# GNN kernel, two attention passes: a third message buffer, and a group's three messages ahead of the next scores

## The reference, cut to what matters

```python
def gat_conv(x, src, dst, W, a_src, a_dst, b):      # HEADS = 8, HEAD_DIM = 32
    h = (x @ W).reshape(N, HEADS, HEAD_DIM)
    e = (h * a_src).sum(-1)[src] + (h * a_dst).sum(-1)[dst]
    e = where(e > 0, e, 0.2 * e)
    m = segment_max(e, dst)
    ex = exp(e - m[dst])
    out = segment_sum(h[src] * ex, dst) / segment_sum(ex, dst)
    return out.reshape(N, HEADS * HEAD_DIM) + b
```

## Time and profile before

| what | value |
|---|---|
| median of 3 runs | 8510.54 us (8506.95 to 8514.32) |
| the profiled execution's own time | 8508.31 us |
| its span, first to last instruction | 8506.5 us |
| granted TensorE clock, mean | 0.829 of full speed |
| first attention pass, start of its first differences | 5810.10 us |
| second attention pass, end of its last combine | 8466.37 us |

### The profile page before, as it was taken

One profiled execution on the slowest core, in us unless ns is written; L12 is line 12 of the kernel. 1 busy time (PEld: TensorE's weight loads), 2 busy tenths in 40 slices (PEclk: granted clock), 3 DMA queues, 4 the chain that ended last, 5 costly groups with the idle time before them and its releaser, 6 DMA issues. The chain is left out here.

```text
span 8506.5 us, 114405 instructions
## 1 busy us (share of the span) xinstructions
PE 6048.5 (71%) x25008; PEld 4478.6 (53%) x25009; DVE 5060.9 (59%) x9534; ACT 2517.1 (30%) x5684; POOL 4108.7 (48%) x4374
## 2 busy tenths in 40 slices
PE   3877787846366667699999999945666664666665
PEld 1446666644244445366666666634555553555554
DVE  4249999952433332466666666655666665666666
ACT  0135555514000001233333333333333332333332
POOL 0037777710377772144444444406666652666663
PEclk9989989878687775899999999966777776777777
DMA  3258888850233331243434334314444442444443
GB/s 119 110 180 261 261 262 260 259 124 4 69 105 105 105 105 37 96 120 113 118 117 119 117 117 120 113 36 138 140 138 127 136 120 74 132 133 137 135 124 91
DMA packets 440380, 1100.31 MB, mean 129 GB/s; under 512 B 102512, under 2 KB 177365, under 8 KB 439479
## 3 DMA queue, kind: packets, MB, share of 16 engines
q0 software_dynamic: 249344, 763.23, 32.1%
q1 hardware_dynamic: 190636, 333.56, 11.8%
HBM read 1014.51 MB, written 81.94 MB: 129 GB/s over the span
## 5 line engine op out<-in xcount | busy, mean ns | idle before, releaser
L765 POOL DMA_INDIRECT st_rows<-g_table,st_stage_idx x1632 | 1561.0, 956 | 881.3 <-issue 457.0
L2475 PE MATMUL st_psM<-st_msg,st_hot 128*128 128x273 f32 x3264 | 958.0, 454 | 310.8 <-DVE st_msg L2322 234.6
L872 POOL DMA_INDIRECT st_rows<-kv_table,st_stage_idx x832 | 841.0, 1011 | 347.6 <-issue 242.5
L705 POOL DMA_INDIRECT st_rows<-p_table,st_stage_idx x816 | 855.3, 1048 | 303.0 <-issue 220.4
L2475 PEld LDWEIGHTS st_psM<-st_msg,st_hot 128*128 128x128 f32 x3264 | 711.3, 223 | 512.9 <-issue 200.1
L765 POOL DMA_INDIRECT st_rows<-h_table,st_stage_idx x816 | 776.6, 952 | 244.5 <-issue 236.3
L1601 DVE TENSOR_TENSOR st_pre<-st_psP,st_rows 128x512 f32<-128x512 f32 x816 | 523.9, 683 | 534.0 <-PE st_psP L1692 393.1
L1698 PE MATMUL st_psC<-st_w,st_rT 128*128 128x256 f32 x3264 | 814.6, 392 | 0.0
L1698 PEld LDWEIGHTS st_psC<-st_w,st_rT 128*128 128x128 f32 x3264 | 587.2, 190 | 373.7 <-ACT st_rT L1659 212.3
L1508 PE MATMUL st_psM<-st_rows,st_hot 128*128 128x256 f32 x1632 | 506.1, 479 | 381.9 <-DMA st_rows<-h_table,st_stage_idx 187.8
L1654 ACT ACTIVATE st_gate<-st_pre 128x256 f32<-128x256 f32 x816 | 340.3, 417 | 1283.9 <-DVE st_pre L1601 1283.9
(11 more groups left out here) (400 smaller groups left out, 11397.9 us busy)
## 6 DMA issues: line engine op xcount, KB each, us to landing
st_dst_row<-in_dst_row SPq DMA_DIRECT2D x310, 512.0 KB, 5.8
kv_table<-st_rows_out SPq DMA_DIRECT2D x25, 1560.0 KB, 5.6
st_ea<-in_ea SPq DMA_DIRECT2D x103, 256.0 KB, 3.8
st_rows<-g_table,st_stage_idx POOLq DMA_INDIRECT x1632
st_pens<-pen_table SPq DMA_DIRECT2D x208, 72.0 KB
st_rows<-kv_table,st_stage_idx POOLq DMA_INDIRECT x832, 5.0
st_rows<-h_table,st_stage_idx POOLq DMA_INDIRECT x816
st_rows<-p_table,st_stage_idx POOLq DMA_INDIRECT x816, 3.7
```

Of the source, the lines that this page charges most:

```text
L705: pool.indirect_dma_start(out=rows[:, u * SLOTS + j, :], out_offset=None, in_=table, in_offset=bass.IndirectOffsetOnAxis(ap=stage_idx[:, u ...
L765: pool.indirect_dma_start(out=rows[:, slot, j, :], out_offset=None, in_=table, in_offset=bass.IndirectOffsetOnAxis(ap=stage_idx[:, g, u * ...
L872: pool.indirect_dma_start(out=rows[:, slot, j, :], out_offset=None, in_=kv_table, in_offset=bass.IndirectOffsetOnAxis(ap=stage_idx[:, g, u ...
L2475: last = nc.tensor.matmul(out[:, 0:MSG_W], onehots[:, j, :], msg[:, n, j, :], start=(j == 0), stop=(j == SLOTS - 1))
```

## The change

`st_msg` gets a third buffer, one for each supertile of a group, and `st_diff` a second. On DVE, the differences of the next group come ahead of the third combine, and all three messages of the next group behind it, ahead of the next edge scores; the loop's branch stands behind the messages. On ACT, the weights of the next group stand behind the factors of the third supertile, with a wait for the one-hots ahead of them (they share a PSUM bank with the columns that `make_hot` reads), and the three pairs of message columns stand together at the head of a group. On PE, the second scatter follows the first, then come the transposes of the scores, and the extras' sums move back: that of the first supertile behind the transposes, that of the second behind `turn_back`. After each `expand` a matmul of two zero columns carries the semaphore, so that DVE needs no count of extras there. `work_of` is split in two: DVE loads the blocks of three supertiles at once at the head of a group, and the bounds of an extra's loop only where there is one.

```diff
+    def blocks_of(eng, row, count=1):
+
+        _, values = nc.values_load_multi_w_load_instructions(
+            work[0:1, ds(row, count), 2:4], engines=[eng.engine], min_val=0, max_val=NS * NB,
+            skip_runtime_bounds_check_because=BOUNDED)
+        return [(values[2 * n], values[2 * n + 1]) for n in range(count)]
...
-            msg = st.sb("msg", [P, 2, SLOTS, MSG_W])
+            msg = st.sb("msg", [P, U, SLOTS, MSG_W])
-            diff = st.sb("diff", [P, SLOTS, U, H3])
+            diff = st.sb("diff", [P, 2, SLOTS, U, H3])
+            zeros = st.sb("zeros", [P, 2], F32R)
...
-                        _, x1, _, _ = work_of(dve, U * q + U)
                         dve.wait_ge(S["expanded"], START + U * q + U)
-                        dve.wait_ge(S["x_expanded"], START + x1)
...
-                    def combine(s, n, ahead, ahead_u):
-                        x0, x1, b0, more = work_of(dve, s + 1)
+                    def combine(s, n, ahead, ahead_u, block):
+                        b0, more = block
...
-                        n = slot % 2
-                        dve.wait_ge(S["summed"], START + s - 1)
-                        v.tensor_tensor(msg[:, n, :, GAT_W:GAT_W + H3], group_view(psW)[:, :, u, :],
+                        dve.wait_ge(S["summed"], START + s - 2)
+                        v.tensor_tensor(msg[:, u, :, GAT_W:GAT_W + H3], group_view(psW)[:, :, u, :],
...
-                    def group(i, g, ahead):
+                    def differences(i, g):
                         q = 2 * i + g
+                        dve.wait_ge(S["back_ps"], START + q + 1)
+                        hold(dve, held)
+                        v.tensor_tensor(diff[:, g, :, :, :], et[:, :, :, :], group_view(psW), ALU.subtract).then_inc(S["diffed"], 1)
+
+                    def early_messages(i, g):
+                        messages(i, g, 0)
+                        messages(i, g, 1)
+                        messages(i, g, 2)
+
+                    def group(i, g, ahead, blocks):
                         s = 6 * i + U * g
                         link.turn()
-                        dve.wait_ge(S["back_ps"], START + q + 1)
-                        v.tensor_tensor(diff[:, :, :, :], et[:, :, :, :], group_view(psW), ALU.subtract).then_inc(S["diffed"], 1)
-                        messages(i, g, 0)
                         if ahead:
-                            dve.wait_ge(S["diffed"], START + q + 1)
+                            dve.wait_ge(S["diffed"], START + 2 * i + g + 1)
                             edge_scores(i + g, 1 - g)
-                        messages(i, g, 1)
-                        combine(s, g % 2, s + U, 0)
-                        messages(i, g, 2)
+                        combine(s, g % 2, s + U, 0, blocks[0])
                         if ahead:
                             segment_maxima(i + g, 1 - g)
-                        combine(s + 1, (g + 1) % 2, s + U + 1, 1)
-                        combine(s + 2, g % 2, s + U + 2, 2)
+                        combine(s + 1, (g + 1) % 2, s + U + 1, 1, blocks[1])
+                        if ahead:
+                            differences(i + g, 1 - g)
+                        combine(s + 2, g % 2, s + U + 2, 2, blocks[2])
+                        if ahead:
+                            early_messages(i + g, 1 - g)
 
                     v.memset(NODE[:, :, :], 0.0)
                     v.memset(best[:, :, :], -BIG)
+                    v.memset(zeros[:, :].bitcast(F32), 0.0).then_inc(S["zeroed"], 1)
...
+                    differences(0, 0)
+                    early_messages(0, 0)
                     with dve.Fori(0, TURNS - 1) as i:
                         for g in range(2):
-                            group(i, g, True)
...
                     def message_columns(i, g, u):
                         slot = U * g + u
                         s = 6 * i + slot
-                        act.wait_ge(S["combined"], START + s - 1)
+                        act.wait_ge(S["combined"], START + s - 2)
                         hold(act, held)
-                        nc.scalar.activation(msg[:, slot % 2, :, MSG_W - 1], first[:, ds(s * SLOTS, SLOTS)], ACT.Copy, scale=RAISE)
+                        nc.scalar.activation(msg[:, u, :, MSG_W - 1], first[:, ds(s * SLOTS, SLOTS)], ACT.Copy, scale=RAISE)
                         nc.scalar.activation(
-                            msg[:, slot % 2, :, 0:GAT_W].rearrange("p j (h c) -> p j h c", h=H3)[:, :, :, HW3 - 1],
-                            diff[:, :, u, :], ACT.Exp).then_inc(S["msg_cols"], 1)
-
-                    def group(i, g, ahead):
+                            msg[:, u, :, 0:GAT_W].rearrange("p j (h c) -> p j h c", h=H3)[:, :, :, HW3 - 1],
+                            diff[:, g, :, u, :], ACT.Exp).then_inc(S["msg_cols"], 1)
+
+                    def weights(i, g):
+                        act.wait_ge(S["diffed"], START + 2 * i + g + 1)
+                        hold(act, held)
+                        act.wait_ge(S["onehot"], START + 6 * i + U * g + U)
+                        nc.scalar.activation(group_view(psU), diff[:, g, :, :, :], ACT.Exp).then_inc(S["weights"], 1)
+
+                    def group(i, g, ahead, last=False):
                         q = 2 * i + g
                         s = 6 * i + U * g
-                        act.wait_ge(S["diffed"], START + q + 1)
-                        nc.scalar.activation(group_view(psU), diff[:, :, :, :], ACT.Exp).then_inc(S["weights"], 1)
                         message_columns(i, g, 0)
                         message_columns(i, g, 1)
+                        message_columns(i, g, 2)
                         make_factors(s)
                         if ahead:
                             make_hotrow(q + 2, 0)
-                        message_columns(i, g, 2)
                         if ahead:
                             make_hotrow(q + 2, 1)
+                        make_factors(s + 1)
+                        if ahead:
                             make_hotrow(q + 2, 2)
-                        make_factors(s + 1)
                         make_factors(s + 2)
+                        if not last:
+                            weights(i + g, 1 - g)
                         if ahead:
                             make_extra_hotrows(q + 2)
 
...
-                        bring(hotrow[:, u, :, :], block_number(b0), u == 0).then_inc(S["expanded"], 1)
+                        bring(hotrow[:, u, :, :], block_number(b0), u == 0)
                         with pe.If(more):
+                            x0, x1 = extras_of(pe, s + 1)
                             with pe.Fori(x0, x1) as x:
                                 pe.wait_ge(S["x_hotrow"], START + x + 1)
                                 bring(xhotrow, block_number(b0 + 1 + x - x0), False).then_inc(S["x_expanded"], 1)
-
-                    def sum_up(out, onehots, n):
+                        at = u * 2 * H3
+                        nc.tensor.matmul(psE[:, at:at + 2], hotrow[:, u, 0, :], zeros[:, :], start=False, stop=True,
+                                         skip_group_check=True).then_inc(S["expanded"], 1)
...
                         scatter(s, 0, g % 2)
-                        scatter_extra(s, g % 2)
+                        scatter(s + 1, 1, (g + 1) % 2)
                         if next_scores:
                             turn_scores(q + 1)
-                        scatter(s + 1, 1, (g + 1) % 2)
-                        scatter_extra(s + 1, (g + 1) % 2)
+                        scatter_extra(s, 0)
                         scatter(s + 2, 2, g % 2)
                         if next_scores:
                             turn_back(q + 1)
-                        scatter_extra(s + 2, g % 2)
+                        scatter_extra(s + 1, 1)
+                        scatter_extra(s + 2, 2)
                         if next_rows:
                             for u in range(U):
                                 expand(q + 2, u)
 
+                    pe.wait_ge(S["zeroed"], START + 1)
```

More of the change, by code:

```diff
@@ L738, in work_of, with extras_of @@
         return at_least_zero(eng, values, NS * NB)
+    def extras_of(eng, row):
+        _, values = nc.values_load_multi_w_load_instructions(
+            work[0:1, ds(row, 1), 0:2].squeeze(1), engines=[eng.engine], min_val=-1, max_val=NS * NB,
+            skip_runtime_bounds_check_because=BOUNDED)
+        return at_least_zero(eng, values, NS * NB)
+    def blocks_of(eng, row, count=1):
+        _, values = nc.values_load_multi_w_load_instructions(
+            work[0:1, ds(row, count), 2:4], engines=[eng.engine], min_val=0, max_val=NS * NB,
+            skip_runtime_bounds_check_because=BOUNDED)
+        return [(values[2 * n], values[2 * n + 1]) for n in range(count)]
     def block_number(b):
@@ L2303, in combine @@
                         with dve.If(more):
+                            x0, x1 = extras_of(dve, s + 1)
                             with dve.If(more - 1):
@@ L2387, in make_extra_hotrows @@
```

(20 more changed lines are left out.)

24 lines of the change are left out of this document (13 added, 11 removed).

## The result

The changed kernel takes 8309.51 us (median of 4 runs, 8301.32 to 8314.22) against 8508.75 (8499.17 to 8514.32): a ratio of 0.9766, 95% interval 0.9749 to 0.9783. The forecast was 8312.

A forecast was written before the change was run, and what follows sets the result against it. A chain between engines, not any engine's load, was taken as the bound. Group heads and bodies summed to 1078.9 us per 32 groups, 84 and 112 us less; 8508.3 − 196 = 8312, own range 8270 to 8350, stated range 8235 to 8420.

The forecast's parts named there:

- The sum: Both passes: 32 groups take 1078.9 us each, 84 and 112 us less, together 196, giving 8312.
- head and body: Parts of a group's period: previous third combine to first combine (forecast 11.9 to 18.7 us), then to third combine (13.3 to 20.0).
- The stalls: Loop branches of DVE and ACT: stalls taken as gone or covered; a 3.3 us stall costs at most 3.3.
- rival B: Loop branches: ACT's and DVE's second stalls stay, costing 65 us in the first pass, 15 in the second; 8390, chance 0.17.
- a rule whose block size was wrong: Loop branches: targets outside two blocks of 256 instructions must be fetched; ACT's loops and DVE's second would fit, ending stalls.
- The messages: Group's head: three messages hide behind PE's 6.43 us first scatter; two extra ahead of edge scores cost 4.84 us.
- C: Gathered rows come late: DVE waits 4 us in half of the 68 groups, +136 us, about 8448; chance 0.07.
- E: PE's clock: the second scatter stays slow, 6.43 us not 3.86; at 3.9 us a group, 8575; chance 0.05.
- F: PE idles less, so the first scatter takes 3.86 us, 2.6 less; half the gain taken, 8246; chance 0.10.
- D: Extras' sums come later, 69 us in 14 first-supertile groups; the head's gain is given back, about 8500; chance 0.05.
- c + 20.0: Body of a group with a first-supertile extra: third combine's end of the span, 20.0 us after first combine c.

The follow-up runs named there:

- after_fit34: The changed kernel with 34 idle increments ahead of ACT's loop in the second pass; 8305.56 us, ratio 0.9761 to the kernel before.
- after_pe_order: after_fit34 with PE's old order of sums, extras and transposes; 8201.84 us, ratio 0.9641 to the kernel before.

## Why the prediction was right

**The sum.** The forecast was 1078.9 us for 32 groups in either pass; 1076.83 and 1086.92 were measured. Walking one group through four engines with durations of the earlier trace rows gave the periods to 0.1 us (no extra), 0.9 (first supertile), 0.8 (second) and 0.2 (third), with the errors of head and body mostly of opposite sign. That the sum is off by only 2.1 us in the first pass is luck in part: the seven groups of the first kind were forecast 6.0 us too long together, the eight of the second 6.7 too short.

**The stalls** (rival B). ACT's went from the first pass and DVE's second one from the second, as the sum took them. In the second pass a new one of ACT came, 39.5 us of "issue" that the forecast had excluded, by a rule whose block size was wrong. It cost some 7 us (1086.92 with it, 1080.09 without it in after_fit34), with 3 us of difference between the same runs in the first pass, where neither has it. Three heads of groups with an extra of the second supertile took 17.4 to 17.6 us with the stall and 15.4 without.

**The messages** are hidden behind the first scatter's 6.43 us as said: where nothing is ahead the head is 12.4 us and DVE waits 1.3 of them (forecast: PE at 11.9, DVE at 11.75). With an extra ahead it mostly waits 3.4 to 4.6 us, where up to 6.4 was forecast.

**C** (late rows): 12.0 us in 2 places; the slack was there. **E and F** (PE's rate): pairs take 6.43 + 3.86 as before, the clock is 0.76; neither shows.

**D was half right, and the sum hid it.** The mechanism named there is real: an extra's sum that comes 4.9 us later in the 14 groups with one of the first supertile. It was priced at 69 us, which makes 8381 and not the "about 8500" of that rival; after_pe_order measured 60 in these groups, and 44 more in the groups without such an extra, whose scans wait for the transposes behind the second scatter, which no rival priced. The forecast's c + 20.0 held the cost, but against the kernel before, whose body was 19.0 on the mean, it looked like 1 us. With the rest of the change in place and PE's old order it is 15.2.

Part by part the 199 us are: -78 for stalls of the kernel before that idle instructions remove as well; about -229 for early messages, third buffer, early weights, the table load out of ACT's loop, DVE's first stall and the blocks loaded at once (8430.8 to 8201.8 on two chips, not taken apart further); +104 for PE's order (102 by the ratios); +4, within the error, for ACT's new stall. The steps are those between the kernels that ran; taken in another order they need not be the same. A right total said nothing of this.

## What to carry to other kernels

Price each part of a change against the same new kernel without that part, not only the whole against the kernel before: a total can be right while one of its parts loses a third of what the others gain. Where an engine waits for a sum, as DVE did here for the extra's, make it ahead of one that nobody needs yet, even if PE then has to wait. And when "issue" stands at a loop's branch in one copy of the code and not in the other, count where the loop begins and ends before reordering work: here idle instructions ahead of the loops were worth 78 us, with nothing reordered.

## What was not expected of the hardware

The queue whose packets follow the loops moves instructions in packets of 8192 bytes (370 packets, 3.03 MB, before; 282 and 2.30 MB in after_fit34); a second one has 30 packets of 16,384. Idle instructions ahead of the loops (102 and 158 on DVE, 6 on ACT) took 0.9% off the time. The same program takes 8.51 ms on three chips and 10.15 ms on two others, and a change that gains 2.3% on the first is, in its near relatives, 1.2 to 2.5% slower on the second.
